# Moving half of the other batch's finished tiles from the first loop to the second loop, in the last block of a fused attention and expert kernel

## The reference, cut to what matters

```
xn = layernorm(x)                                  # x: 4 batches x 2048 rows x 256
s  = linear attention of xn per batch:             # heads 16
     Q, K, V = layernorm(xn @ W + b); phi = tanh(. @ Wphi + b) + 1
     alpha = softmax(mean(Q) . K); KV = sum(phiK * alpha * V)
     attn = phiQ @ KV / (phiQ @ sum(phiK * alpha))
     attn = layernorm(attn + 0.1 * grouped_conv(attn))
     s = attn + gelu(attn @ W1 + b1) @ W2 + b2 + xn
f  = causal attention, then 16 experts, top 2, of xn, both with residuals
out = x + s * silu(f)
```

## Time and profile before

| | |
|---|---|
| median of 3 runs | 2038.44 us (2034.1 to 2043.3) |
| profiled execution | 2036.94 us, span 2035.2 us |
| mean granted clock of PE | 0.951 of full speed |
| PE busy | 1805.6 us (89%) |
| DVE busy | 1370.6 us (67%) |
| POOL busy | 961.6 us (47%) |
| ACT busy | 818.9 us (40%) |

### The profile page before, as it was taken

How to read it: one execution, slowest core, us unless ns; L and a number is a source line. 1 busy time by engine, 2 the same in 40 slices (tenths; PEclk the granted TensorE clock), 3 DMA queues, 4 the chain that set the end, 5 groups by cost and what they waited for, 6 DMA issues and landing times. The chain is left out here.

```text
span 2035.2 us, 37234 instructions
## 1 busy us (share of the span) xinstructions
PE 1805.6 (89%) x12776; PEld 1615.9 (79%) x12776; DVE 1370.6 (67%) x3573; ACT 818.9 (40%) x1945; POOL 961.6 (47%) x1500
## 2 busy tenths in 40 slices
PE   2699998299999998996999999999868999998998
PEld 1477776275898867995999999999856699975998
DVE  2698885653566535553777777777558488795786
ACT  1466664164233453231333333333247233472432
POOL 4466663066456465552656566566333133340431
PEclk7799998599999999998999999999979999999999
DMA  4454432123434123233333333332136012362121
GB/s 113 176 179 173 173 137 71 44 69 109 144 122 138 61 87 138 95 131 101 95 124 119 106 116 121 100 118 72 53 110 205 25 53 79 100 186 63 53 72 56
DMA packets 163510, 218.29 MB, mean 107 GB/s; under 512 B 22874, under 2 KB 144931, under 8 KB 161294
## 3 DMA queue, kind: packets, MB, share of 16 engines
q1 hardware_dynamic: 140574, 166.61, 25.5%
q0 software_dynamic: 18464, 49.49, 6.9%
q10 hardware_dynamic: 4304, 0.02, 0.1%
HBM read 114.94 MB, written 107.22 MB: 109 GB/s over the span
## 5 line engine op out<-in xcount | busy, mean ns | idle before, releaser
L1804 POOL DMA_INDIRECT picked_d<-h,home x160 | 162.7, 1017 | 193.1 <-DVE h L1849 158.6
L1731 ACT ACTIVATE hid<-bank 128x512 f32<-128x512 f32 x160 | 95.6, 597 | 333.7 <-PE bank L130 333.7
L128 PE MATMUL bank<-rows_hi,up_hi 128*128 128x256 f32 x640 | 189.0, 295 | 10.0 <-POOL up_lo L1798 7.7
L130 PE MATMUL bank<-rows_hi,up_lo 128*128 128x256 f32 x640 | 182.4, 285 | 0.0
L129 PE MATMUL bank<-rows_lo,up_hi 128*128 128x256 f32 x640 | 182.3, 285 | 0.0
L130 PE MATMUL bank<-down_hi,hid_lo 128*128 128x256 f32 x640 | 181.1, 283 | 0.0
L128 PE MATMUL bank<-down_hi,hid_hi 128*128 128x256 f32 x640 | 181.1, 283 | 0.0
L129 PE MATMUL bank<-down_lo,hid_hi 128*128 128x256 f32 x640 | 181.1, 283 | 0.0
L1138 POOL DMA_INDIRECT buf_d<-lt,to_row x128 | 134.2, 1048 | 85.5 <-POOL lt L1134 41.7
L1437 PE MATMUL bank<-wconv,knt 128*128 128x128 f32 x1280 | 154.5, 276 | 0.0
L1863 DVE TENSOR_TENSOR hid_lo<-hid,hid_hi 128x512 fp32r<-128x512 f32 x160 | 113.2, 715 | 56.5 <-ACT hid_hi L1731 53.2
(11 more groups left out here) (307 smaller groups left out, 5581.3 us busy)
## 6 DMA issues: line engine op xcount, KB each, us to landing
buf_d<-zeros SPq DMA_DIRECT2D x16, 1360.0 KB, 7.1
rows_in<-buf_d SPq DMA_DIRECT2D x80, 272.0 KB, 2.8
lt<-ln_d SPq DMA_DIRECT2D x128, 128.0 KB, 2.2
picked_d<-nothing SPq DMA_DIRECT2D x32, 512.0 KB, 3.3
job_picked<-picked_d SPq DMA_DIRECT2D x64, 256.0 KB, 2.9
x<-in_x SPq DMA_DIRECT2D x16, 512.0 KB, 4.3
after_d<-after SPq DMA_DIRECT2D x16, 512.0 KB, 2.9
ln_d<-ln SPq DMA_DIRECT2D x16, 512.0 KB, 2.9
```

The costliest lines, as they stand in the source:

```text
L128: pe.matmul(dst, hi, mhi, start=start and i == 0, stop=False)
L130: mm = pe.matmul(dst, lo, mhi, start=False, stop=end)
L1731: act.activation(dst[:, 2 * half:2 * half + 2].rearrange("p f c -> p (f c)"), bank[half][:], ACT.Gelu_apprx_tanh).then_inc(e_hid, 1)
L1804: pool.indirect_dma_start(picked_d, bass.IndirectOffsetOnAxis(home[i % TAG_RING][:, r:r + 1], axis=0), h2[p][:, r], None, bounds_check=PIC ...
```

## The change

Of each batch's sixteen jobs on tiles of batches 0 and 1, eight (SOON) stay in the first loop, every second step: the mix at steps 4, 6, ..., 18, the join and the silu at 5, 7, ..., 19. The other eight go to the second loop, one per pair, ahead of the pair's two own jobs: its mix behind the gelu splits before the two own mixes, its join (`join_other`) before the `sout` of the pair's first tile. The order of jobs is thus eight others, then eight times other, own, own. Since SP's loads for batch 3 hang on the job number, its first two loads of x now follow job 8 in place of job 15.

```diff
+        SOON = BT - PAIRS_A
...
                 def own(b, n):
-                    return job_of(b, BT + n)
+                    return job_of(b, SOON + (PAIR + 1) * (n // PAIR) + 1 + n % PAIR)
+
+                def other(b, n):
+
+                    return job_of(b, n if n < SOON else SOON + (PAIR + 1) * (n - SOON))
...
-                                if job == BT - 1:
+                                if job == SOON:
                                     load_x(first + 1, 0)
                                     load_x(first + 1, 1)
...
-                            if not scatters and 0 <= i - LATE - 2 < BT:
-                                silu(job_of(b, i - LATE - 2))
+                            j = i - LATE - 2
+                            if not scatters and j % 2 == 0 and 0 <= j // 2 < SOON:
+                                silu(other(b, j // 2))
...
                             if not scatters and 0 <= k < BT and k % PAIR == PAIR - 1:
+                                silu(other(b, SOON + k // PAIR))
                                 silu(own(b, k - 1))
...
+                        def join_other(job):
+                            dve.wait_ge(job_s_in[job % RING], 16 * s_loads(job))
+                            join(job, job_s[job % RING])
...
-                            if not scatters and 0 <= j < BT:
-                                job = job_of(b, j)
-                                dve.wait_ge(job_s_in[job % RING], 16 * s_loads(job))
-                                join(job, job_s[job % RING])
-                            if not scatters and 0 <= j + 1 < BT:
-                                mix(job_of(b, j + 1))
+                            if not scatters and j % 2 == 0 and 0 <= j // 2 < SOON:
+                                join_other(other(b, j // 2))
+                            if not scatters and j % 2 == 1 and 0 <= (j + 1) // 2 < SOON:
+                                mix(other(b, (j + 1) // 2))
...
                                 if not scatters:
+                                    mix(other(b, SOON + g))
                                     mix(own(b, k - 1))
                                     mix(own(b, k))
                             k = i - 6
                             if 0 <= k < BT and k % PAIR == PAIR - 1:
+                                if not scatters:
+                                    join_other(other(b, SOON + k // PAIR))
```

More of the change, by code:

```diff
@@ L963, in own @@
                 def own(b, n):
-                    return job_of(b, BT + n)
+                    return job_of(b, SOON + (PAIR + 1) * (n // PAIR) + 1 + n % PAIR)
+                def other(b, n):
+                    return job_of(b, n if n < SOON else SOON + (PAIR + 1) * (n - SOON))
                 def is_own(job):
-                    return job % EACH >= BT
+                    j = job % EACH - SOON
+                    return j >= 0 and j % (PAIR + 1) > 0
                 def batch_tile(job):
                     b, j = batches[job // EACH], job % EACH
-                    return b * BT + j - BT if is_own(job) else (b - 2) * BT + j
+                    if j < SOON:
+                        return (b - 2) * BT + j
+                    pair, r = (j - SOON) // (PAIR + 1), (j - SOON) % (PAIR + 1)
+                    return b * BT + pair * PAIR + r - 1 if r else (b - 2) * BT + SOON + pair
                 def rounds(job):
```

## The result

The changed kernel was slower: 2056.12 us in the median of 5 runs (2045.62 to 2060.03) against 2038.44; the ratio is 1.0071, 95% interval 1.0049 to 1.0093. The forecast was 2043.5 in a range of 2030 to 2058.

The account below looks back on a forecast made before the run. PE was taken to set the pace in both loops. Costs of 20.0 less gains of 13.4 gave +6.6 on the profiled 2036.94, which lies 1.5 below the median: 2043.5 us, range 2030 to 2058.

Parts of the forecast that it names:

- The gains of batch 2's first loop: Batch 2's first loop: gains of 1.3, 2.4, 3.7 and 1.7 us from taking jobs out, 9.1 together.
- 1.3 at the stall: Batch 2's first loop, where DVE waits for x: one join fewer shortens PE's idle of 4.65 by 1.3 us.
- 3.7 at the tail: End of batch 2's first loop: DVE reaches the mean of q 4.2 earlier, removing PE's wait of 3.68; gain 3.7 us.
- 1.7 of L1383: L1383 at batch 2's end: without the idle ahead the clock stays up, 7.03 instead of 8.72; gain 1.7 us.
- I take the clock as kept: After batch 2's x stall: with idle cut to 3.4, PE keeps full clock; gain 2.4 us, 0 as the other end.
- the DVE work itself just fits: Second loop: a third mix and join, 2.1 us, against DVE's idle of 2.27 per pair; period 18.0 by work alone.
- The wait on x: Second loop's steady pairs: x lands 3.0 after issue, DVE stalls 1.2; 1.1 us more per pair, 8.8 over eight.
- Batch 2's other pairs: Batch 2's second loop: pair 0 costs 2.5 us, pair 4 3.0 plus 2.4 for the clock, pair 5 nothing, pair 6 0.3.
- From pair 7 to batch 3's pair 0: Batch 2's pair 7 costs 3.0 us; batch 3's first loop gains 3.2 at its tail and 1.1 on ACT's qkn.
- the 1.1 for ACT's qkn: Early in batch 3's first loop: PE's wait for ACT's qkn goes as ACT gets half its silus; gain 1.1 us.
- x is not late: Rival, second loop: x lands within about 2.2, the eight pairs cost 0.3 each; −7, about 2030 us; chance 0.17.
- x is late by much more: Rival, second loop: landing about 3.9 or slow SP issues, 2.4 per pair, periods 20 or more; +21, about 2058; chance 0.21.

Follow-up runs that it names:

- e8: The changed kernel run once more, with nothing altered; ratio to the kernel before 1.0054.
- e6: The changed kernel with job_x issued first after each store and job places picked by traces, ten in the first loop, six in the second; 2027.43 us, ratio 0.9942.
- e2: The changed kernel with SP issuing job_x first after each store, ahead of job_picked, job_after and job_s; 2029.78 us, ratio 0.9963.
- e7: The changed kernel with job_x issued second after each store, behind job_picked alone; ratio 0.9964.
- e3: The kernel before with the first loop thinned as in the change and the other eight jobs of each batch left out; 2027.08 us, ratio 0.9957.

## Why the prediction came out as it did

The direction of the sum and its mechanism held, and the time lies in the range, but near its end: +15.1 in place of +6.6. The likeliest outcome by the forecast, within 0.5%, did not come; the range reached as far as 2056 only because it took in the rival of a later x, so that the time fell into it is in part luck. By the forecast's own terms, with the second block cut where PE starts the second product of batch 2's pairs 0 and 7 and of batch 3's pair 0:

- **The gains of batch 2's first loop**, forecast 9.1, came to 6.7 (1637.77 − 1485.38 = 152.4 before, 1624.67 − 1478.96 = 145.7 now). The 1.3 at the stall, 3.7 at the tail and 1.7 of L1383 held. The step that failed is "I take the clock as kept": after an idle of 3.42 PE ran at 0.50 as before, which is the whole 2.4. (In e8 this stretch gave 4.0: the clock fell there once more, for 6.8 us in the attention of batch 2.) Taking 3.15 and 3.68 as the two sides of a bound was wrong: PE idled 2.38 at this place in e6, and the clock fell there too.
- **The added DVE work**, "the DVE work itself just fits": shown by e2, periods of 18.1 to 18.3.
- **The wait on x**, 1.1 per steady pair: the eight pairs took 1.6, 2.2, 1.6, 1.9, 1.2, 1.4, 3.2 and 1.4 more, 14.5 in place of 8.8. The mechanism was right, the size off, mostly by the landing: 3.0 was taken, 3.5 was the middle of the measured ones (3.4 by the profile's own landing). Put into the forecast's own cycle, 0.5 more gives 1.6 per pair, the value of six of the eight to within 0.4. The 3.2 is a landing of 5.2 and a stretch at half clock behind it. The 2.2 and the 1.9 are late issues: one load ahead on SP took longer, and x went out 2.5 behind the store in place of 1.88. e8 repeats the sum, 15.7. The row taken, 3.1, was of an x in the first loop, behind which SP issued nothing for 1.8 us; in the pair the own tile's store and the next load of 256 KB are issued within a microsecond of it. Why 3.1 became 3.4 was not tried. That the place in SP's order counts is shown: 3.4 as the fifth, 2.7 as the second (e7), 2.2 as the first (e2). The Trainium skill's fit ("DMA: Bandwidth & Descriptors", section "Anatomy of one DMA — SWDGE (gpsimd) path"), an estimate of 2.3 for these bytes, is given for transfers that GpSimd issues, and these are issued by SP; it lies below all thirteen and near the 2.2 of e2, where nothing but the store stands ahead of x. The rows decide.
- **Batch 2's other pairs**: pair 0 cost 1.7 (forecast 2.5), pair 4 3.7 (5.4), pair 5 2.2 (0), pair 6 0.3 (0.3). The 5.8 for pairs 4 and 5 together is about the 5.4 of the forecast: its half-clock stretch fell partly into the pair behind.
- **From pair 7 to batch 3's pair 0**: forecast −1.3, measured +0.2 (137.58 against 137.34). PE waited 2.90 for ant_lo as foreseen (3.0), the 3.15 before the scores and the 1.1 for ACT's qkn went; but the clock fell twice where before it held: right behind the wait for ant_lo, and in the sums over k and v. Compared instruction by instruction with the kernel before, PE lost some 1.4 and 1.2 us there. The two stretches:

```profile
1776.30:1779.70 3.40, 3.40 (x11) 2.74 (x11) 2.40 (x11) 2.01 (x8) 1.54 (x4) 0.51 0.87 256
1857.90:1862.00 4.10, 4.10 (x21) 3.97 (x21) 1.89 (x5) 0.55 (x1) 0.00 (x0) 0.58 0.00 0
```

- **Batch 3's last pairs**, forecast 0: 0.4 and 0.2, and 1.5 were won back in the last one, where the clock had been at half for 3.4 us before and now held.

The rival "x is not late" fell with the first timeline. The rival "x is late by much more" named what happened in kind: the pairs cost 1.8 in the mean, between my 1.1 and its 2.4, without a landing of 3.9 as a rule; three of their periods, 20.3, 20.1 and 21.4, passed its sign of 20. That the slower side had 0.32 and "within 0.5%" 0.60 had two reasons. The larger is the price of the eight pairs, 5.7 of the 8.5 that the sum missed: it hung on one landing of 3.0, and late issues on SP and a stretch at half clock came on top. The other is the clock, whose losses I treated as single terms: some of the stalls that the late x made were followed by half clock, and I priced that at one pair only.

What e2 shows beyond: the forecast's 13.4 of gains was near (12.3 in e3), though not in all its terms, and most of it (9.5) was within reach of the change by moving two lines in SP's order.

## What to carry to other kernels

When work moves within a ring of buffers, look first at what the ring's order now asks for late: here a third mix and a third join per pair cost 2.8 us or less in all, and the load that they pushed behind a store some 20. The remedy was in the issue order of one queue: the transfer that somebody waits for goes out first, those for the next round behind it. And price a landing by rows with the same place in the order and the same neighbours, and each new stall with a chance of half clock behind it.

## What the runs showed that I had not expected

- Half clock after short idle times: behind idles of 2.27 (e2), 2.38 (e6) and 2.96 (e3) at the stall the granted clock fell, for example:

```profile
1518.80 0.41 PE L1333 MATMUL bank<-ident,xnb 128*128 128x128 f32 x2 [2.27 <-DVE ant_lo L1535]
```

```profile
1518.80:1522.80 4.00, 3.38 (x9) 2.59 (x10) 3.86 (x15) 3.69 (x12) 1.67 (x4) 0.57 0.00 0
```

One of 3.15 in the kernel before was not followed by it. Behind the shorter idles at the stall the half-clock stretch was shorter: 1.7 us in the estimate for e2, e3 and e6, 3.4 before and in the change.
- The same kernel loses different amounts to the clock from one execution to the next: 20.2 and 24.3 in the two profiles of the change. In e2, e3 and e6, where the wait before the scores of batch 3 is gone, half-clock stretches appear some 15 to 40 us later that the kernel before does not have there.
- One issue on SP is not always 0.43 us: 1.52 for an x in e2, up to 2.13 in e8, and what SP issues behind a slow one goes out later: in pair 2 of the change a load of job_picked took 1.10, and x was issued 2.52 after the store in place of 1.88.
